# Four graph layers on one core: layer 0's weights used in two parts, unit 0's norms applied by two engines, dummy turns in 16 gaps, and other orders of the work

## What is computed

```python
x = layernorm(x + graph_attention(x, W, a, beta, adj))      # layer 0
x = layernorm(x + (adj @ x) @ weight + bias)                # layer 1
x = layernorm(x + masked_attention_8_heads(x, qkv, proj, gamma, beta, adj))  # layer 2, with a norm of its own inside
x = layernorm(x + gated_recurrence_3_steps(x, adj, w3, w4, w5, u3, u5))      # layer 3

# layer 0
h = x @ W;  s1 = h @ a[:256];  s2 = h @ a[256:]
e = leaky_relu(s1[:, :, None] + s2[:, None, :]) * adj
out = elu(softmax(e) @ h + beta * h)
```

## Time and profile before

| | |
|---|---|
| runs | 1384.9, 1385.81, 1387.71 us, median 1385.81 |
| the profiled execution's own time | 1390.11 us |
| its span in the trace | 1388.3 us |
| mean granted clock of TensorE | 0.987 |
| TensorE busy (matmul) | 1345.8 us, 97% of the span, 10447 instructions |
| VectorE busy | 1057.0 us, 76% |
| ScalarE busy | 783.7 us, 56% |
| GpSimd busy | 134.2 us, 10% |
| chain that ended last | TensorE 91%, VectorE 6%, ScalarE 2%, issue 1% |

### The profile page before, as it was taken

How to read it: one execution, slowest core, us unless ns; L and a number is a source line. 1 busy time by engine, 2 the same in 40 slices (tenths; PEclk the granted TensorE clock), 3 DMA queues, 4 the chain that set the end, 5 groups by cost and what they waited for, 6 DMA issues and landing times.

```text
span 1388.3 us, 26972 instructions
## 1 busy us (share of the span) xinstructions
PE 1345.8 (97%) x10447; PEld 1143.7 (82%) x10447; DVE 1057.0 (76%) x2371; ACT 783.7 (56%) x1449; POOL 134.2 (10%) x194
## 2 busy tenths in 40 slices
PE   7879999999999999999999999999999999999996
PEld 6768888888888888888888888888888888887785
DVE  5776878877787887778787787887778877868465
ACT  3536556656465565656646565664656556564453
POOL 4000101000010100100000010100001010010000
PEclk8979999999999999999999999999999999999998
DMA  5001010000000000000000000000000000010000
GB/s 176 9 1 39 1 24 32 17 13 25 23 30 23 30 15 8 30 23 30 23 30 8 15 30 23 30 15 23 15 23 30 23 31 1 9 38 20 27 1 30
DMA packets 54670, 34.53 MB, mean 25 GB/s; under 512 B 34912, under 2 KB 51552, under 8 KB 54624
## 3 DMA queue, kind: packets, MB, share of 16 engines
q1 hardware_dynamic: 52816, 29.43, 7.1%
q0 software_dynamic: 1248, 3.94, 0.9%
q10 hardware_dynamic: 560, 0.52, 0.1%
HBM read 12.92 MB, written 8.39 MB: 15 GB/s over the span
## 4 chain that ended last, share of the span: by engine, by line
PE 91%; DVE 6%; ACT 2%; issue 1%; DMA 0%; POOL 0%; POOLq 0%; DVEq 0%; ACTq 0%
PE banks L122 22%; PE banks L124 21%; PE banks L123 21%; PE banks L651 8%; PE banks L646 4%; PE banks L812 2%; PE banks L714 2%; PE banks L797 2%; PE banks L914 2%; PE banks L786 2%; PE banks L698 1%; PE banks L775 1%; PE banks L706 1%; DVE l_s L2243 0%; DVE late_lo L2217 0%
## 5 line engine op out<-in xcount | busy, mean ns | idle before, releaser
L1574 ACT ACTIVATE l_r<-banks,bias_r 128x512 f32<-128x512 f32 x90 | 61.5, 683 | 182.3 <-PE banks L124 182.3
L1591 ACT ACTIVATE banks<-banks,bias_h 128x512 f32<-128x512 f32 x96 | 63.5, 662 | 107.0 <-PE banks L124 106.5
L262 POOL TENSOR_TENSOR l_rstd<-l_mv,eps 128x4 f32<-128x4 f32 x47 | 18.3, 389 | 877.2 <-DVE l_mv L256 877.2
L2217 DVE TENSOR_TENSOR l_rh_lo<-l_r,l_rh_hi 128x512 fp32r<-128x512 f32 x90 | 60.7, 687 | 52.9 <-ACT l_rh_hi L1440 51.7
L276 ACT ACTIVATE y<-l_sum,l_offset,l_rstd 128x256 f32<-128x256 f32 x128 | 71.1, 595 | 11.8 <-DVE l_offset L270 11.8
L122 PE MATMUL banks<-l_rh_hi,u_hi 128*128 128x512 f32 x180 | 75.2, 418 | 0.7 <-DVE l_rh_lo L2217 0.7
L1440 ACT ACTIVATE l_rh_hi<-l_r 128x512 fp32r<-128x512 f32 x90 | 54.0, 630 | 36.5 <-DVE l_r L2460 36.5
L1585 ACT ACTIVATE banks<-banks,bias_z 128x512 f32<-128x512 f32 x96 | 62.9, 656 | 17.7 <-PE banks L124 17.7
L124 PE MATMUL banks<-l_rh_lo,u_hi 128*128 128x512 f32 x180 | 71.1, 395 | 0.0
L123 PE MATMUL banks<-l_rh_hi,u_lo 128*128 128x512 f32 x180 | 70.8, 394 | 0.0
L651 PE MATMUL banks<-adj_t,y 128*128 128x128 f32 x544 | 69.5, 277 | 0.5 <-ACT y L276 0.2
(11 more groups left out here) (304 smaller groups left out, 4331.9 us busy)
## 6 DMA issues: line engine op xcount, KB each, us to landing
x_tok<-in_x_dram SPq DMA_DIRECT2D x15, 512.0 KB, 3.5
l_res<-y SPq DMA_DIRECT2D x15, 512.0 KB, 3.0
out_dram<-l_res SPq DMA_DIRECT2D x15, 512.0 KB, 3.0
l_vpair<-l_vstage SPq DMA_DIRECT2D x32, 128.0 KB, 3.2
w_raw<-in_L_gnn_w_w_dram POOLq DMA_DIRECT2D x3, 512.0 KB, 7.7
qkv_raw<-in_L_gnn_w_qkv_dram POOLq DMA_DIRECT2D x1, 768.0 KB, 4.4
l_res<-in_x_dram SPq DMA_DIRECT2D x1, 512.0 KB, 5.1
u_raw<-in_L_gnn_u_w_dram POOLq DMA_DIRECT2D x2, 256.0 KB, 7.7
```

Of the source, the lines that this page charges most:

```text
L1574: nc.scalar.activation(own(u).r[:, m, :], rz(u)[:, m, :], ACT.Tanh, scale=0.5, bias=w.biases["r"][:, m:m + 1]).then_inc(s.r_ready.of(u), 1)
L1591: nc.scalar.activation(hv(u)[:, m, :], hv(u)[:, m, :], ACT.Tanh, bias=w.biases["h"][:, m:m + 1]).then_inc(s.hv_ready.of(u), 1)
L2217: return nc.vector.tensor_tensor(parts[1][:, k, :], bank, parts[0][:, k, :].bitcast(F32), ALU.subtract)
```

## The change

- Layer 0's W is split and used in two parts. `sum_a` waits for W and a alone (beta gets a semaphore of its own). Columns 0 to 255 and the two columns W a are split by separate instructions (`high_columns`, `high_l0`, `low_columns`, `low_l0`). For unit 0 `l0_project` makes 256 columns, and `project_columns` makes the two others of all four tiles with 24 matmuls of two columns, into a corner of another bank; `take_columns` copies them out. `l0_diagonal(0)` waits for these and the constants. VectorE's first instructions are now `sum_a` 0 to 2, `l0_low(0, 0)`, `sum_a(3)`, `l0_low(0, 1)`, `low_columns`, `make_constants`, `take_columns`, `l0_diagonal(0)`, `low_l0`.
- Unit 0's norms of layers 0, 1 and 2 are applied by two engines: tiles 0 and 1 on ScalarE, 2 and 3 on VectorE (`apply_here`). Who reads y0, y1, y2 of unit 0 waits for both (`past_y`).
- Dummy turns stand in 16 places of TensorE's fill: 12, 22, 3, 7, 3, 4, 10, 3, 5, 5, 5, 12, 9, 5, 4 and 4 of them, 113 in all where 38 were, each place with a bank of its own.
- SyncE loads x of unit 2 behind the swap of unit 0; GpSimd adds the biases before unit 0's first root.
- All orders of the fill, of the body and of the drain, on TensorE, ScalarE and VectorE, are new.

```diff
@@ load_weights, Weights
-        load(act, 0, w.a_raw[:, :, :], p.a["L0_gnn_a"].rearrange("(j f) o -> o j f", j=2).to_broadcast([P, 2, DIM]))
-        load(act, 0, w.beta[:, :], on_all_partitions("L0_gnn_beta", 1))
+        act.dma_start(w.a_raw[:, :, :], p.a["L0_gnn_a"].rearrange("(j f) o -> o j f", j=2).to_broadcast([P, 2, DIM])
+                      ).then_inc(w.sems["a_loaded"], 16)
+        load(act, 4, w.beta[:, :], on_all_partitions("L0_gnn_beta", 1))
@@ fused
+    def past_y(eng, n, u):
+
+        if isinstance(u, int) and u < 0:
+            return
+        eng.wait_ge(*(s.y0, s.y1, s.y2)[n].at(u, 1))
+        if is_first(u):
+            eng.wait_ge(s.halves_applied, n + 1)
@@ SyncE fill
             l0_load(1)
+            l2_swap(0)
             l0_load(2)
-            l2_swap(0)
+            l2_swap(1)
+            l0_load(3)
             l3_keep(0)
-            l0_load(3)
-            l2_swap(1)
             l0_load(4)
@@ TensorE
+        def project_columns():
+
+            pe.wait_ge(ws["columns_ready"], 1)
+            pe.wait_ge(*s.l0_lo.at(0, CH))
+            for t in range(TILES):
+                ins = rows_by_weights(s_columns[:, t, :], b.early, t, w.l0, slice(DIM, WX))
+            ins.then_inc(ws["l0_columns"], 1)
@@ TensorE body
             l3_u(i, 0, 1)
             l3_r(i, 0, 0)
-            l3_r(i, 0, 1)
             l3_w(i, 0, 1)
             l2_turn_prob(i + 1, 0)
+            l3_r(i, 0, 1)
             l2_turn_prob(i + 1, 1)
...
             l3_w(i, 2, 0)
             l2_turn(i + 2, 0)
+            l3_diff(i, 2, 0)
             l2_turn(i + 2, 1)
+            l3_diff(i, 2, 1)
             l3_w(i, 2, 1)
-            l3_diff(i, 2, 0)
+            l2_project(i + 2, 0)
             l3_candidate(i, 2, 0)
-            l2_project(i + 2, 0)
+            l2_project(i + 2, 1)
             l3_candidate(i, 2, 1)
-            l2_project(i + 2, 1)
-            l3_diff(i, 2, 1)
             l2_values(i + 2)
@@ TensorE fill, to layer 1 of unit 0
-            keep_busy(12)
+            keep_busy(12, X[:, 3, :])
             for n in range(2):
                 l0_turn(0, n)
-            keep_busy(5)
-            l0_turn(1, 0)
+            keep_busy(22, X[:, 3, :])
             turn_adj()
-            l0_turn(1, 1)
-            keep_busy(3)
+            project_columns()
+            for n in range(2):
+                l0_turn(1, n)
+            keep_busy(3, X[:, 3, :])
+            l0_spread(0)
             for n in range(4):
                 l0_project(0, n)
-            l0_spread(0)
-            keep_busy(18)
+            keep_busy(7, Y[:, 2, :])
             l0_turn_att(0)
+            keep_busy(3, X[:, 3, :])
             for n in range(2):
                 l0_attend(0, n)
-            for n in range(2):
+            for n in range(4):
                 l0_project(1, n)
             turn_gate(0)
-            for n in range(2, 4):
-                l0_project(1, n)
+            l0_spread(1)
             turn_gate(1)
-            l0_spread(1)
+            keep_busy(4, X[:, 1, :])
             for n in range(2):
                 l1_aggregate(0, n)
@@ TensorE drain, unit 14's first step
             l3_w(14, 0, 1)
+            l3_candidate(14, 0, 0)
             l3_diff(14, 0, 0)
-            for n in range(2):
-                l3_candidate(14, 0, n)
+            l3_candidate(14, 0, 1)
             l3_diff(14, 0, 1)
             for n in range(2):
                 l3_turn(14, 0, n)
-            f_turn(15, 0)
+            for n in range(2):
+                l3_aggregate(14, 0, n)
@@ VectorE
+        def apply_here(n, t):
+
+            norm, z, y = ((l0, b.s, b.y0), (l1, b.l1_sum, b.y1), (l2o, b.l2_sum, b.y2))[n]
+            if t == 2:
+                dve.wait_ge(*norm.offset_ready.at(0, 1))
+            ins = nc.vector.tensor_scalar(y[:, t, :], z[:, t, :], norm.rstd[:, t:t + 1], norm.offset[:, t:t + 1],
+                                          op0=ALU.mult, op1=ALU.add)
+            if t == TILES - 1:
+                ins.then_inc(s.halves_applied, 1)
@@ VectorE body, end of layer 3's second step
             l3_gated(i, 1, 0)
             l3_difference(i, 1, 1)
-            l1_variance(i + 2)
+            l3_gated(i, 1, 1)
             l3_update(i, 1, 0)
-            l3_gated(i, 1, 1)
             l3_update(i, 1, 1)
@@ VectorE fill, between unit 0's layer 0 and unit 1's scores
             l0_variance(0)
-            low_l1()
+            l0_diagonal(1)
+            low_qkv()
+            l0_scores(1)
             l0_offset(0)
-            l0_diagonal(1)
+            for n in range(2, 4):
+                l0_apply(0, n)
+            l0_leaky(1)
```

More of the change, by code:

```diff
@@ L1062, in fill @@
                 l1_product(1, n)
-            l2_turn_prob(0, 0)
-            l0_turn(2, 0)
-            for n in range(1, 4):
-                l2_turn_prob(0, n)
-            l0_turn(2, 1)
-            for n in range(4):
-                l2_attend(0, n)
+            keep_busy(5, Y[:, 1, :])
+            for n in range(2):
+                l0_turn(2, n)
+            keep_busy(12, Y[:, 3, :])
             for n in range(4):
@@ L1072, in fill @@
             for n in range(2):
+                l2_turn_prob(0, n)
+            l0_spread(2)
+            l2_turn_prob(0, 2)
+            l2_attend(0, 0)
+            l2_turn_prob(0, 3)
+            for n in range(1, 4):
+                l2_attend(0, n)
+            keep_busy(9, Y[:, 3, :])
+            l0_turn_att(2)
+            keep_busy(5, Y[:, 3, :])
+            for n in range(2):
                 l2_turn_o(0, n)
-            l0_spread(2)
-            for n in range(4):
-                l2_output(0, n)
-            l0_turn_att(2)
             for n in range(2):
@@ L1097, in fill @@
             l3_w(0, 0, 0)
-            for n in range(3):
+            for n in range(2):
                 l2_turn_prob(1, n)
+            l3_diff(0, 0, 0)
+            l2_turn_prob(1, 2)
+            l2_attend(1, 0)
+            l2_turn_prob(1, 3)
+            for n in range(1, 4):
+                l2_attend(1, n)
             l3_w(0, 0, 1)
-            l2_turn_prob(1, 3)
-            for n in range(4):
-                l2_attend(1, n)
-            l3_diff(0, 0, 0)
             l3_candidate(0, 0, 0)
@@ L1204, in drain @@
+            for n in range(2):
                 l1_product(14, n)
             l3_diff(12, 1, 0)
-            f_turn(13, 0)
+            for n in range(2, 4):
+                l1_product(14, n)
+            for n in range(2):
+                l3_w(12, 1, n)
+            for n in range(2):
+                l3_candidate(12, 1, n)
+            l3_diff(12, 1, 1)
+            for n in range(2):
+                f_turn(13, n)
             for n in range(2):
                 f_aggregate(13, n)
-            f_turn(13, 1)
@@ L1738, in fill @@
             l0_exp_v(1, 0)
-            for n in range(4):
+            for n in range(2):
                 l1_apply(0, n)
+            high_gate(2)
             for n in range(2):
@@ L2019, in drain @@
             l3_update_gate(13, 1, 1)
             l3_high(13, 1, 0)
-            for n in range(2):
-                l2_take_qk(15, n)
+            l2_take_qk(15, 2)
             l3_high(13, 1, 1)
@@ L3138, in drain @@
-            l3_low(14, 1, 0)
-            l3_update(14, 1, 1)
-            l3_low_rh(15, 1, 0)
-            l3_reset(15, 1, 1)
-            l3_low_rh(15, 1, 1)
-            l3_low(14, 1, 1)
+                l3_low_rh(15, 1, n)
+            for n in range(2):
+                l3_low(14, 1, n)
             l3_difference(15, 1, 0)
-            l3_gated(15, 1, 0)
-            l3_low_a(14, 1, 0)
-            l3_update(15, 1, 0)
             l3_low_a(14, 1, 1)
             l3_difference(15, 1, 1)
+            l3_gated(15, 1, 0)
@@ L3160, in drain @@
             l3_gated(14, 2, 0)
+            l3_difference(14, 2, 1)
             l3_update(14, 2, 0)
-            l3_low_a(15, 1, 1)
-            l3_difference(14, 2, 1)
-            for n in range(2):
-                l3_reset(15, 2, n)
-            l3_gated(14, 2, 1)
-            l3_low_rh(15, 2, 0)
-            l3_update(14, 2, 1)
-            l3_low_rh(15, 2, 1)
-            for n in range(2):
-                l3_residual(14, n)
+            l3_gated(14, 2, 1)
+            l3_update(14, 2, 1)
```

1407 lines of the change are left out of this document (739 added, 668 removed).

## The result

The changed kernel took 1384.93 us (median of 21 runs, 1382.72 to 1386.07), the kernel before 1387.79 us (21 runs, 1381.92 to 1391.14): a ratio of 0.998, 95% interval 0.9972 to 0.9989. It is faster by 2.9 us, where 8.1 were forecast. The time lies in the range of 8 in 10 (1369 to 1386.5), but outside the forecast's own range (1372 to 1383) and above the 1377.7 that it names; by the prediction's own bounds it is a case of "the same" (1383.0 to 1388.6), to which it gave 0.12. The gain is off by almost a factor of three.

A forecast was written before the change was run, and what follows sets the result against it. TensorE's own instructions bound the loop, chains over VectorE, ScalarE and GpSimd the fill. Fill -15.1, put-off work +2, hand-overs +2, loop +3 and drain 0 sum to -8.1 us: median 1377.7, range of 8 in 10 1369 to 1386.5.

The forecast's parts named there:

- The path of unit 0: Fill, unit 0's chain from first load to layer 3: diagonal 4.6 us earlier, layer 2's projection 7.6 earlier.
- hand-overs: Fill: some 60 hand-overs in the chain, 0.03 to 0.05 us each, partly rounded away: +2 us, bounds 0 and 4.
- What is put off: Unit 2's residual, exponential part and statistics on VectorE, now behind unit 1's maxima: +2 us, bounds 0 and 4.2.
- -15.1: Fill: layer 3 of unit 0 starts 15.1 us earlier, at 100.9 us.
- The norm on two engines: Unit 0's norms in the fill: two tiles each on ScalarE and VectorE, -1.0 us for each of three norms.
- The clock, -1.8 and -5.3: Fill at full clock through dummies: -1.8 us for unit 0's attention, -5.3 for the work of 90 to 110 us.
- The loop, +3: Loop: two more changes of kind at 0.11 us over 11 trips, +2.4, and a later h, +0.6.
- The drain, 0: Drain: unit 14's wait stays, lost cover +1, longer cover for other candidates -1; 0 us, bounds -3 and +3.
- More than forecast: Rival: changes of kind vanish in TensorE's queue and put-off work finds cover, 1371 us; chance 0.18.
- The second: Rival, the gain ends at unit 0: late dummies or a clock falling despite them lose the 5.3, 1383 us; chance 0.18.
- The lock: Rival: on the ports shared by VectorE and GpSimd, `low_qkv` holds unit 0's root up, 1.4 us less gain, 1379.1; chance 0.04.
- The slower rival: Rival: a loop operand that had cover comes late in each trip; 1.5 us late gives 1394 us; chance 0.08.

The follow-up runs named there:

- b_same: The kernel before, unchanged, run again: 1385.98 us, ratio 0.9999.
- b_dummies: The kernel before with more dummy turns in TensorE's fill and nothing else changed: 1382.62 us, ratio 0.9965.
- a_noswap: The changed kernel with, in TensorE's loop, the fourth turning of probabilities put ahead of the first attend: 1380.98 us, ratio 0.9955.
- a_oldbodydrain: The changed kernel with the loop's and drain's orders of before on all five engines, so the new fill alone: 1377.7 us, ratio 0.994.
- a_newdrain: The new fill and new drain around the old loop, differing from a_oldbodydrain by the drain's orders alone: 1380.52 us, ratio 0.9952.
- a_grouped: The changed kernel with layer 2's four turnings, then four attends, grouped again in TensorE's loop: 1393.69 us, ratio 1.0052.
- n_pebody: a_oldbodydrain with TensorE's new loop order beside the other engines' old ones: 1409.71 us, ratio 1.0161.

## Why the prediction was right and wrong

**The path of unit 0: right, step by step.** Forecast and measured: diagonal 13.0 to 13.5 and 14.19; attention turned 18.5 and 19.94; layer 1 at 31.4 and 32.24; layer 2's projection 47.8 and 48.38; unit 2's attention 76.6 and 77.59; layer 3 at 100.9 and 101.75. The lag begins ahead of the diagonal, with two terms. The 24 products of two columns take 2.68 us, 0.11 each, where I took 0.07 between bounds of 0.03 and 0.23; each has a weight load of its own, and the loads start 0.11 us apart. And they start at 11.05, right behind the 22 dummies, though VectorE had the columns' low part ready at 10.31: the dummies lie 0.7 us in the path, which the working left out. Layer 3 came 0.85 us after 100.9, so less than half of the 2 us set aside for hand-overs was used, as I read it because the durations of rows overlap by about as much as the hand-overs take.

**What is put off, +2: wrong.** It cost nothing: from layer 3's start to the loop's first mask it is 81.08 us before and 81.11 after. VectorE is busy 68.50 of 86 us from 110 on, so there was cover enough. The fill therefore gave 14.2 us in the trace, where -15.1 + 2 + 2 = -11.1 were forecast.

**The norm on two engines, three times -1.0: oversized.** The first is 0.98, as worked out; the second is 0.35 and the third 0.4. By then, as I read the order, unit 0's norm is no longer alone on the path: ahead of the turning that needs it TensorE has a gate's turning to end in the second case and unit 1's scores in the third.

**The clock, -1.8 and -5.3: right for that execution, wrong for the median.** This is the step that failed most: a price that was read in one execution, of 1390.11 us, was taken off the median of others. The granted clock was 1.00 in the first 110 us, as forecast, and in this trace both terms were won. But both were read from one execution, 2.3 us above the median of 21 runs, whose falls at 95 to 105 us were deeper than those in the profile of `b_same`; and the changed kernel's own profiled execution lay 1.9 us under its median. The working took 8.1 us from the median of 1385.81 although it knew that its execution stood 4.3 us above it, and that difference was itself clock that other executions had not lost. These 4.2 us are what separates the 7.1 us of the two traces from the 2.9 of the medians: 1390.11 - 1387.79 = 2.32, and 1384.93 - 1383.02 = 1.91. In the medians the clock is worth less: dummies alone give 4.5 us (`b_dummies`), where these two terms had 7.1. The new fill also has falls of its own in some executions, at 10 to 20 us (five profiles of kernels with it), and the changed kernel's profile has one behind the drain's wait.

The account of the 5.2 us between forecast and median is then: 4.2 from the two executions, and 1.0 from the other terms together, with the fill 3.1 better than forecast, the loop 2.6 worse and the drain 1.5 worse. That the terms come so near to cancelling is luck.

**The loop, +3: right in kind, half in size.** The mechanism was changes of kind on TensorE, and it is what the runs show. But I priced each at 0.11 and counted two: this is the other step that failed. The turning put between two attends costs 0.27 to 0.30 (the change back included, and taken out again by `a_noswap`, 0.28); the product between two turnings another 0.16 (1.47 + 0.41 + 1.49 us for 1.40 + 0.41 + 1.40), some 0.1 comes between 41 and 46 us behind the mask, where unit i+1's turnings and aggregations for layer 3 alternate once more and a candidate's product follows an aggregation; the split turn of layer 2, which I had counted, costs next to nothing (its eight turnings and the two products beside them take 3.67 us against 3.65). In sum 0.53 us a trip instead of 0.27, and over twelve steps 5.6 us net instead of 3.0 (6.5 beside `a_oldbodydrain`, whose first trip is 0.8 shorter than that of the kernel before). The changed order also gains nothing there: there was no wait to win but 0.67 us in seven trips, and it is not seen in the difference.

**The drain, 0: 1.5 us too good.** 1.09 from mask to mask are the drain's own orders (`a_newdrain` has them too); 0.4 behind it is a gain of 0.7 (141.2 us without a fall, in `a_newdrain`) less 1.1 of the fall that follows the wait in this execution. The wait for unit 14's h stayed, as forecast, at 2.2 us.

**The rivals.** More than forecast (1371) is not what happened, although one of its conditions (put-off work under cover) was. The second has most of the truth in another form: not that the clock falls in spite of dummies, but that it falls less in the kernel before than my execution had it. The lock did not come: the addition of unit 0's root had ended when `low_qkv` began at 28.90 us; its power, from 28.77 on, ran beside `low_qkv`, and they took 1.04 and 1.76 us, their usual lengths. The Trainium skill's page "SBUF — State Buffer", section "SBUF: two separate sides", would have one of them wait for the other in full; this trace shows no such wait for that pair. The slower rival, an operand late in every trip, did not come either, but `a_grouped` and `n_pebody` show how near it is: one line moved on one engine makes it 0.8 us a trip.

That the new orders of loop and drain turn a gain of 8.1 us into 2.9 is shown by `a_oldbodydrain` (0.994 against 0.998), and that the loop has most of it by the masks (the eleven trips make 5.9 of 7.3 us). What is not settled is which of the fill's new orders makes which part of the 3.5 us that are left beside the dummies (0.994 against 0.9965), the split norms among them; the columns of their own were not tried alone.

## What to carry to other kernels

Before a gain is priced from one profiled execution, see how the executions differ: here time follows the mean granted clock from 1381.7 at 0.995 to 1391.4 at 0.986, and a term read from a low-clock stretch of one of them is worth its average over all, not its value there. Where TensorE is busy all of a loop's trip, its order is a cost of its own: price each place where turnings, attends and full products alternate from rows that show that very pair, since here one such place took 0.28 us in each of eleven trips. And put short dummy turns into TensorE's waits first: in the kernel before that alone brought 0.35%.

## What the runs showed of the hardware that was not expected

GpSimd's 128x4 addition of the root takes 0.20 us at its shortest (41.67 in the changed kernel). In two places where it began after a two-input instruction of VectorE it ended when that one ended. GpSimd's and VectorE's timelines of the changed kernel:

```profile
71.05 0.55 POOL L264 TENSOR_TENSOR l_rstd<-l_mv,eps 128x4 f32<-128x4 f32 x1 [18.52 <-DVE l_mv L258]
...
88.35 1.09 POOL L264 TENSOR_TENSOR l2i_rstd<-l2i_mv,eps 128x4 f32<-128x4 f32 x1 [15.67 <-DVE l2i_mv L258]
89.52 1.01 POOL L267 TENSOR_TENSOR l2i_rstd<-l2i_rstd,minus_half 128x4 f32<-128x4 f32 x1
```

```profile
70.89 0.66 DVE L2230 TENSOR_TENSOR proj_lo<-proj_raw,proj_hi 128x512 fp32r<-128x512 f32 x1
...
88.19 1.19 DVE L2507 TENSOR_TENSOR l_sum<-l_otok,l_sum 128x1024 f32<-128x1024 f32 x1
89.49 1.69 DVE L2515 SCALAR_TENSOR_TENSOR l_otok<-l_otok,l2i_mv,ln_gamma 128x256 f32<-128x256 f32 x4
```

The addition of 71.05 ends at 71.60, VectorE's subtraction at 71.55; that of 88.35 at 89.44, VectorE's at 89.38. The power that follows it (89.52, 128x4 too) shows nothing of this beside L2515 and takes its 1.01 us. So the lock of the Trainium skill's page "SBUF — State Buffer", section "SBUF: two separate sides", is borne out for the addition, at up to 0.9 us, and not seen for the power.

The clock fell behind TensorE's wait of 2.2 to 2.3 us in the drain in six of the nine profiles with the new fill and no dummies there (the changed kernel's and `a_oldbodydrain`'s among them), and in none of the three with the old fill, though in `a_oldbodydrain` the instructions around the wait are those of before. In the two profiles with dummies that cover the wait in part (2.13 us of dummies, 0.35 and 0.32 left) it stayed at 1.00, as it did in three of the nine without.
